# fp32 x1 product as one fp32r product over 96 stacked rows, and the class product over all 128 rows

## The chip, the cores and the metric

The kernel runs on one core of a Trainium2 chip. The time is the device time of one execution in microseconds (us), the median of three runs. Engines are named as the profile names them: PE (TensorE, matmuls; PEld are its weight loads), DVE (VectorE), ACT (ScalarE), POOL (GpSimd) and SP (SyncE, which issues most DMAs).

## The reference, cut to what matters

`x` has 128 entries of 64 positions and 256 features. Four layers follow one another. The change touches the first one and a table lookup in the last:

```python
def _L0_cond_ref(x, mu, W_dec, b_dec, V):          # K = 30
    U = (mu @ W_dec + b_dec).reshape(B, IN_DIM + 1, K)
    param = jnp.einsum('bik,kj->bij', U, V)
    weight = param[:, :-1, :]
    bias = param[:, -1, :]
    out = jnp.einsum('bsd,bde->bse', x, weight)
    out = out + bias[:, None, :]
    return out
...
x = x + _L0_cond_ref(x, cond_512, ...)             # x1 in the kernel
x = x + _L1_cond_ref(x, cond_512, ...)             # x2
x = _L2_cond_ref(x, ...)                           # x3
...
h = _ln(x, pw_g[pathway_ids], pw_b[pathway_ids])   # in the last layer, _L3_cond_ref
h = _ln(h, cp_g[compartment_ids], cp_b[compartment_ids])
t = _ln(x, tm_g[time_steps], tm_b[time_steps])
s = _ln(x, ms_g[scale_type], ms_b[scale_type])
```

The kernel computes layer 0 as t = x . U (30 values a position) and then x1 = x + t . V.

## The kernel before, in words

The 8192 positions are cut into 16 chunks of 512 (8 entries each). A tile holds either features on its 128 partitions (two blocks of 128 features by 512 positions) or positions (four tiles of 128 positions by 256 features). Setup decodes U for all entries and prepares tables; then each chunk goes through the stages in a software pipeline. Every engine has its own list of stages, written out by hand in `run_slots`: a list for the beginning, an `order` that a loop repeats for each chunk, each stage with a lag (the chunk it works on is the loop's number less the lag), and a list for the end. An engine runs its list strictly in that order and waits on semaphores that other engines raise. PSUM has four tensors of two banks, `ps_a` to `ps_d`, which the stages share in turn.

The stages that matter here, in the order in which a chunk meets them:

- `pe_t` (L919, TensorE): t for the 8 entries, into bank 1 of `ps_b`, four strips of 30 rows at partitions 0, 32, 64 and 96.
- `act_th1` (L1171, ScalarE) copies the four strips side by side into rows 0 to 29 of `t_st`; `act_th2` (L1178) copies those to rows 32 to 61.
- `pe_x1` (L935, TensorE): V times `t_st` into `ps_b`, in fp32. Feature block 0 uses rows 0 to 29, block 1 the copy in rows 32 to 61. The trace shows two passes (records) for each fp32 matmul. `v_x1add` (L1345) adds x.
- `g_style` (L1516, GpSimd) scales x1 into `xm_t`; `pe_l1` (L948) multiplies it in fp32 into `ps_d`; `v_l1mul`, `v_l1min` and `v_x2add` (L1352, L1361, L1367) make x2; `pe_dn` (L962), `v_dnmul`, `v_dnadd`, `act_relu`, `pe_up` (L976) and `v_x3sum` make x3.
- `pe_x3r` (L988) transposes x3, `v_xstat` (L1398) takes its statistics, `g_rootx` and `act_xnorm` normalise it, `g_gather` fetches table rows by an indirect DMA, `g_hmul` and `g_hadd` apply them, `v_hstat`, `g_rooth` and `act_hnorm` (L1209) normalise again.
- `pe_cp` (L1046, TensorE): the class gains as a product of one-hot rows (`onehot`) with `gain_tab`, in bf16, into `ps_d`. The 24 class rows stand twice in both operands, at partitions 0 and 64; position tiles 0 and 1 use the first copy, 2 and 3 the second. `v_hprod` (L1428) multiplies them onto h, `pe_hht` (L994) transposes h into `ps_b`, where t had been.
- The last layer's first product, 3 x 2 fp32r matmuls for each of 8 blocks (L902 to L904: low times high, high times low, high times high), in parts named x3, tm, ms and h; `act_silu`, `act_silh`, `v_sillow`; the second product `pe_w2` (the same lines into `ps_b`); `act_ysquare`, `g_rooty`, `v_ygain`, `v_ynorm` and the store.

"fp32r" is a fp32 type with a shorter mantissa, for which the trace shows one record a matmul; a value is split into a high half (a copy into fp32r) and a low half (value less high half), as the last layer does throughout.

The order of TensorE's loop is `pe_xht` 5, `pe_w1_tm` 6, `pe_up` 4, `pe_w1_ms` 6, `pe_cp` 5, `pe_x1` 3, `pe_w1_h` 6, `pe_x3r` 4, `pe_t` 2, `pe_l1` 3, `pe_hht` 5, `pe_shift` 5, `pe_w1_x3` 5, `pe_tm` 5, `pe_dn` 3, `pe_w2` 6, `pe_ms` 5 (the number is the lag). `pe_hht` waits, among others, for a semaphore that says that t has been read out of `ps_b`:

```python
        def pe_hht(eng, c):
            newest(eng, c, (v_x1, 2), (v_y, -2))
            newest(eng, c, (a_th1, 3), (v_x1, 2), (v_y, -2))
            wait(eng, v_h, c.n + 1)
```

## Time and profile before

| | us |
|---|---|
| median of three runs | 523.61 (521.86 to 524.25) |
| profiled execution, its own time | 521.21 |
| its span in the trace | 519.4 |
| mean granted TensorE clock | 0.994 of full speed |

| engine | busy us | share of the span | instructions |
|---|---|---|---|
| PE | 486.3 | 94% | 3198 |
| DVE | 405.8 | 78% | 696 |
| POOL | 391.0 | 75% | 367 |
| ACT | 336.3 | 65% | 638 |

Busy time of an engine is the time in which at least one of its instructions ran. Matmuls are pipelined: a record's duration holds the time until its last result is out, so the distance from one start to the next, and not the duration, is what a matmul costs in a row of them. The loop repeats every 27.8 us for each chunk in the middle of the span. "Idle" in brackets is time in which an engine had nothing running before an instruction, with the instruction or DMA whose end let it go.

### The profile page before, as it was taken

To read this page: it belongs to the slowest core of one execution; us is meant where nothing else is said; L and a number is where in the kernel's file an instruction comes from. 1 tells how busy PE (TensorE), PEld (TensorE's weight loads), DVE (VectorE), ACT (ScalarE), POOL (GpSimd) and SP (SyncE) were. 2 spreads that over 40 slices of the span, in tenths; PEclk is the share of its full clock that TensorE was granted. 3 is DMA by queue.
4 is the path that set the end of the run, shared out by engine and by line. 5 is a ranking of instruction groups with operands and counts; after the bars stand their busy time and mean duration, and the time that the engine had idled before them with its cause. 6 is when DMAs were issued, how large, how long until landed. Compare 5 with 4: busy or idle time off the path is not lost.

```text
span 519.4 us, 9425 instructions
## 1 busy us (share of the span) xinstructions
PE 486.3 (94%) x3198; PEld 354.2 (68%) x3198; DVE 405.8 (78%) x696; ACT 336.3 (65%) x638; POOL 391.0 (75%) x367
## 2 busy tenths in 40 slices
PE   2987887999999999999999999999999999998993
PEld 2953644767677776768686867677776768687682
DVE  2958876868788788888787878788787888886863
ACT  4573667456767676766777776767676767656832
POOL 6468799889878879697978787788779793787321
PEclk9999999999999999999999999999999999999997
DMA  8887705625252352608080716253442613104102
...
DMA packets 34989, 61.78 MB, mean 119 GB/s; under 512 B 5017, under 2 KB 17413, under 8 KB 34580
## 3 DMA queue, kind: packets, MB, share of 16 engines
...
q8 instruction: 14, 0.23, 0.2%
...
## 4 chain that ended last, share of the span: by engine, by line
PE 79%; POOL 6%; DVE 5%; DMA 4%; issue 3%; ACT 2%; SPq 0%; DVEq 0%; POOLq 0%; ACTq 0%
PE ps_c L902 11%; PE ps_c L904 11%; PE ps_c L903 10%; PE ps_d L948 9%; PE ps_d L962 5%; PE ps_a L976 5%; PE ps_b L902 3%; PE ps_b L903 3%; PE ps_b L904 3%; PE ps_b L935 2%; PE ps_a L988 2%; DMA set_wdec<-in_nets_rows 2%; PE ps_a L994 2%; PE ps_b L994 2%; DMA set_wdec<-in_W_dec 1%
## 5 line engine op out<-in xcount | busy, mean ns | idle before, releaser
L1507 POOL DMA_INDIRECT pw_rows<-in_pw,gidx x64 | 65.0, 1016 | 17.9 <-issue 17.4
L948 PE MATMUL ps_d<-xm_t,l_w 128*128 128x512 f32 x128 | 59.0, 603 | 2.2 <-POOL xm_t L1516 2.2
L1209 ACT ACTIVATE h<-h,nb_h,rstd_h 128x256 f32<-128x256 f32 x64 | 33.3, 591 | 33.1 <-POOL nb_h L1531 33.0
L1240 ACT ACTIVATE tm_t_h<-ps_a 128x1024 fp32r<-128x1024 f32 x16 | 16.4, 1026 | 45.6 <-DVE ps_a L1413 45.6
L1516 POOL TENSOR_TENSOR xm_t<-x_t,style 128x1024 f32<-128x1024 f32 x16 | 30.5, 1905 | 20.2 <-DVE x_t L1345 20.1
L948 PEld LDWEIGHTS ps_d<-xm_t,l_w 128*128 128x128 f32 x128 | 23.1, 190 | 26.8 <-issue 24.2
L1546 POOL TENSOR_TENSOR h<-xhat,pw_rows 128x1024 f32<-128x1024 f32 x16 | 38.0, 2378 | 4.1 <-ACT xhat L1209 4.1
L1565 POOL TENSOR_TENSOR w_up<-up_rep,ugub 128x1024 f32<-128x1024 f32 x16 | 38.0, 2372 | 2.2 <-issue 2.0
L1551 POOL TENSOR_TENSOR h<-h,pw_rows 128x1024 f32<-128x1024 f32 x16 | 38.3, 2394 | 1.3
L1567 POOL TENSOR_TENSOR w_up<-w_up,ugub 128x1024 f32<-128x1024 f32 x16 | 38.1, 2382 | 1.3
L902 PE MATMUL ps_b<-w_h,act_t_l 128*128 128x256 f32 x128 | 37.7, 294 | 0.4 <-DVE act_t_l L1450 0.4
L1577 POOL TENSOR_TENSOR x3be<-x,ln_gb 128x1024 f32<-128x1024 f32 x16 | 37.8, 2364 | 0.0
L1352 DVE TENSOR_TENSOR ps_d<-ps_d,dcoef 128x1024 f32<-128x1024 f32 x16 | 19.7, 1232 | 21.6 <-PE ps_d L948 21.6
L903 PE MATMUL ps_b<-w_l,act_t_h 128*128 128x256 f32 x128 | 36.1, 282 | 0.0
L904 PE MATMUL ps_b<-w_h,act_t_h 128*128 128x256 f32 x128 | 36.0, 281 | 0.0
L1209 ACT ACTIVATE xhat<-ps_a,nb_x,rstd_x 128x256 f32<-128x256 f32 x64 | 31.0, 564 | 6.7 <-POOL nb_x L1531 6.7
L962 PE MATMUL ps_d<-x_t,down_w 128*64 128x256 f32 x256 | 31.2, 385 | 3.0 <-DVE x_t L1367 3.0
L976 PEld LDWEIGHTS ps_a<-act_dn,w_up 128*128 128x128 f32 x256 | 30.5, 191 | 4.9 <-issue 2.6
L976 PE MATMUL ps_a<-act_dn,w_up 128*128 128x128 f32 x256 | 31.6, 277 | 2.2 <-ACT act_dn L1188 1.2
L1590 POOL TENSOR_TENSOR ve_y<-y_var,eps 128x4 f32<-128x4 f32 x15 | 3.0, 202 | 40.2 <-ACT y_sq L1320 40.2
L1418 DVE TENSOR_TENSOR ps_d<-ps_d,xh_t 128x1024 f32<-128x1024 f32 x16 | 19.7, 1231 | 17.4 <-PE ps_d L1031 17.4
L1320 ACT ACTIVATE y_sq<-ps_b 128x256 bf16<-128x256 f32 x64 | 23.7, 380 | 14.8 <-PE ps_b L904 14.8
...
## 6 DMA issues: line engine op xcount, KB each, us to landing
...
pw_rows<-in_pw,gidx POOLq DMA_INDIRECT x64, 3.7
...
```

The costliest lines, as they stand in the source:

```text
L902: eng.matmul(out, wl, ah, start=first, stop=False)
L903: eng.matmul(out, wh, al, start=False, stop=False)
L904: return eng.matmul(out, wh, ah, start=False, stop=last)
L948: m = eng.matmul(ps_l1[:, o, :], l1_w[:, k, o * P:(o + 1) * P], xm_t[:, k, :], start=k == 0, stop=k == KB - 1)
L962: m = eng.matmul(ps_dn[e * HID:(e + 1) * HID, part * CT * S:(part + 1) * CT * S], down_w[:, k, part * HID:(part + 1) * HID], x[:, k, e], s ...
L976: m = eng.matmul(ps_up[:, k, j * P:(j + 1) * P], w_up[:, j, k * P:(k + 1) * P], act_dn[:, j, :, :], start=True, stop=True)
L1209: m = eng.activation(out[:, j, :], src[:, j, :], ACT.Identity, bias=nb[k][:, j:j + 1], scale=rstd[k][:, j:j + 1])
L1507: eng.indirect_dma_start(pw_rows[c.ring][:, j, :], None, t["pw"], bass.IndirectOffsetOnAxis(ap=gidx[c.ring][:, j:j + 1], axis=0)).then_inc ...
L1546: eng.tensor_tensor(h1[:, :, :], xhat[:, :, :], pw_rows[c.ring][:, :, 0:D], ALU.mult).then_inc(g_h1m, 1)
L1551: eng.tensor_tensor(h1[:, :, :], h1[:, :, :], pw_rows[c.ring][:, :, D:2 * D], ALU.add).then_inc(g_h1, 1)
L1565: eng.tensor_tensor(w_up[:, :, :], q, ugub[:, :, 0:D], ALU.mult).then_inc(g_upm, 1)
L1567: eng.tensor_tensor(w_up[:, :, :], w_up[:, :, :], ugub[:, :, D:2 * D], ALU.add).then_inc(g_up, 1)
```

## The change

The fp32 product x1 becomes one fp32r matmul for each feature block, over 96 rows. `t_st` holds t's high half in rows 0 to 29, its low half in rows 32 to 61 and the high half again in rows 64 to 93; `v_st` holds V's high half in rows 0 to 63 and its low half from row 64. One pass then sums high times high, low times high and high times low. `act_th1` writes the high half, `act_th2` the copy of it, and a new stage on VectorE, `v_tlow`, takes the low half: four subtractions of 30 x 128 from the strips in `ps_b`. It stands before `v_l1mul` in VectorE's loop. `pe_x1` waits for both, and `pe_hht`, which overwrites the strips, waits for `v_tlow` in place of `act_th1`. In the setup `act_vhigh` and `v_vlow` split V, and `t_st` is set to zero once (rows 30, 31 and so on are never written).

`pe_cp` uses all 128 rows of `onehot` and `gain_tab`: columns 0 to 255 of `gain_tab` are zero outside the first 24 rows, so its four matmuls no longer use two copies of the class rows. Semaphores are merged where two can be one (`a_th1` into `a_th`, `v_l1u` and `v_l1v` into `v_l1`), with the same waits.

The diff, cut to its core (the semaphore lists and the waits of `v_l1min` and `v_x2add` are left out):

```diff
@@ -148,7 +148,8 @@
         later = sb("later", [CLS, PIECES - 1])
-        v_rep = sb("v_rep", [2 * RP, D])
+        v_rep = sb("v_rep", [PIECES * RP, D])
+        v_st = sb("v_st", [PIECES * RP, D], F32R)
         style = sb("style", [P, KB, B])
@@ -181,7 +182,7 @@
         act_dn = sb("act_dn", [P, CT, 2, S])
-        t_st = sb("t_st", [2 * RP, CH])
+        t_st = sb("t_st", [PIECES * RP, CH], F32R)
 
@@ -406,7 +407,7 @@
         rows_c = rows_of(ps_c)
-        pads = (ubias_p[:, :], act_dn[:, :, :, :], onehot[0][:, :], onehot[1][:, :], shift[0][:, :], shift[1][:, :], gain_tab[:, 2 * D:3 * D],)
+        pads = (ubias_p[:, :], act_dn[:, :, :, :], onehot[0][:, :], onehot[1][:, :], shift[0][:, :], shift[1][:, :], gain_tab[:, :], t_st[:, :].bitcast(F32),)
 
@@ -434,7 +435,7 @@
         def load_weights(eng, c):
-            eng.dma_start(v_rep[:, :], t["V3"][0:2 * RP, :]).then_inc(d_wts, 16)
+            eng.dma_start(v_rep[:, :], t["V3"]).then_inc(d_wts, 16)
             eng.dma_start(down_w[:, :, 0:HID], feat(t["down_p"])).then_inc(d_wts, 16)
@@ -595,6 +596,11 @@
 
+        def v_vlow(eng, c):
+            eng.wait_ge(c_v, 1)
+            low = slice(2 * RP, 3 * RP)
+            eng.tensor_tensor(v_st[low, :], v_rep[low, :], v_st[low, :].bitcast(F32), ALU.subtract).then_inc(c_v, 1)
+
         def v_awmax(eng, c):
@@ -667,8 +673,8 @@
             pick(eng, v_link, gain_tab[0:CLS, :], tab[1][:, :], *(p[:, :] for p in tab_p))
-            eng.scalar_tensor_tensor(gain_tab[STRIP:STRIP + CLS, 0:2 * D], tab_p[2][:, 0:2 * D], masks[:, 2:3],
-                                     tab[1][:, 0:2 * D], ALU.mult, ALU.add).then_inc(v_pick, 1)
+            eng.scalar_tensor_tensor(gain_tab[STRIP:STRIP + CLS, D:2 * D], tab_p[2][:, D:2 * D], masks[:, 2:3],
+                                     tab[1][:, D:2 * D], ALU.mult, ALU.add).then_inc(v_pick, 1)
 
@@ -700,6 +706,10 @@
                               ubias_p[:, e * RP:(e + 1) * RP]).then_inc(d_ub, 16)
+
+        def act_vhigh(eng, c):
+            eng.wait_ge(d_wts, 48)
+            eng.activation(v_st[:, :], v_rep[:, :], ACT.Copy).then_inc(c_v, 1)
 
@@ -929,10 +939,12 @@
             newest(eng, c, (v_y, -4), (v_hl, -3))
-            wait(eng, a_th, c.n + 1)
+            if first(c):
+                eng.wait_ge(c_v, 2)
+            wait(eng, a_th, 2 * c.n + 2)
+            wait(eng, v_thl, c.n + 1)
             for k in range(KB):
-                rows = slice(k * RP, k * RP + RK)
-                m = eng.matmul(ps_x1[:, k, :], v_rep[rows, k * P:(k + 1) * P], t_st[rows, :], start=True, stop=True)
+                m = eng.matmul(ps_x1[:, k, :], v_st[:, k * P:(k + 1) * P], t_st[:, :], start=True, stop=True)
             m.then_inc(p_x1, 1)
@@ -1041,16 +1053,14 @@
             out = rows_of(ps_cp)
-            for j in (0, 2, 1, 3):
-                rows = slice(j // 2 * STRIP, j // 2 * STRIP + CLS)
-                m = eng.matmul(out[:, j, :], onehot[c.ring][rows, j * P:(j + 1) * P], gain_tab[rows, 0:D],
-                               start=True, stop=True)
+            for j in range(CT):
+                m = eng.matmul(out[:, j, :], onehot[c.ring][:, j * P:(j + 1) * P], gain_tab[:, 0:D], start=True, stop=True)
             m.then_inc(p_cp, 1)
...
             newest(eng, c, (v_x1, 2), (v_y, -2))
-            newest(eng, c, (a_th1, 3), (v_x1, 2), (v_y, -2))
+            newest(eng, c, (v_thl, 3), (v_x1, 2), (v_y, -2))
             wait(eng, v_h, c.n + 1)
@@ -1164,18 +1174,20 @@
 
+            if first(c):
+                eng.wait_ge(z_pad, len(pads))
             wait(eng, p_t, c.n + 1)
...
                     "r (q s) -> r q s", s=S), ACT.Copy)
-            m.then_inc(a_th1, 1)
+            m.then_inc(a_th, 1)
 
...
 
-            wait(eng, a_th1, c.n + 1)
-            eng.activation(t_st[RP:RP + RK, :], t_st[0:RK, :], ACT.Copy).then_inc(a_th, 1)
+            wait(eng, a_th, 2 * c.n + 1)
+            eng.activation(t_st[2 * RP:2 * RP + RK, :], t_st[0:RK, :].bitcast(F32), ACT.Copy).then_inc(a_th, 1)
 
@@ -1337,6 +1349,15 @@
 
+        def v_tlow(eng, c):
+
+            wait(eng, a_th, 2 * c.n + 1)
+            high, out = (t_st[lo:lo + RK, :].rearrange("r (q j s) -> r q j s", j=4, s=S) for lo in (0, RP))
+            for j in range(4):
+                src = ps_t[j * RP:j * RP + RK, 0:2 * S].rearrange("r (q s) -> r q s", s=S)
+                m = eng.tensor_tensor(out[:, :, j, :], src, high[:, :, j, :].bitcast(F32), ALU.subtract)
+            m.then_inc(v_thl, 1)
+
         def v_x1add(eng, c):
@@ -1648,7 +1669,7 @@
...
-                             (act_turn, 12), (act_turn, 13), (act_turn, 15), (act_style, 0), (act_dg, 0),
+                             (act_turn, 12), (act_turn, 13), (act_turn, 15), (act_style, 0), (act_dg, 0), (act_vhigh, 0),
...
@@ -1685,23 +1706,23 @@
-                             (v_stylesq, 0), (v_softmax, 0), (v_dceps, 0), (v_dcrcp, 0), (v_x1add, 0),
-                             (v_mostat, 0), (v_w1sum, 0), (v_l1mul, 0), (v_l1min, 0), (v_x2add, 0), (v_monorm, 0),
+                             (v_stylesq, 0), (v_softmax, 0), (v_vlow, 0), (v_dceps, 0), (v_tlow, 0), (v_dcrcp, 0), (v_x1add, 0),
+                             (v_mostat, 0), (v_w1sum, 0), (v_l1mul, 0), (v_l1min, 0), (v_x2add, 0), (v_tlow, 1), (v_monorm, 0),
...
-                             (v_classes, 0), (v_l1mul, 1), (v_l1min, 1), (v_x2add, 1), (v_rows, 0), (v_dnmul, 1),
+                             (v_classes, 0), (v_l1mul, 1), (v_l1min, 1), (v_x2add, 1), (v_tlow, 2), (v_rows, 0), (v_dnmul, 1),
...
-                             (v_xstat, 1), (v_l1mul, 2), (v_l1min, 2), (v_x2add, 2), (v_tmprod, 0), (v_hlow, 0),
+                             (v_xstat, 1), (v_tlow, 3), (v_l1mul, 2), (v_l1min, 2), (v_x2add, 2), (v_tmprod, 0), (v_hlow, 0),
...
-                      order=[(v_x1add, 3), (v_hprod, 5), (v_xstat, 4), (v_sillow, 6), (v_l1mul, 3), (v_l1min, 3),
+                      order=[(v_x1add, 3), (v_hprod, 5), (v_xstat, 4), (v_sillow, 6), (v_tlow, 2), (v_l1mul, 3), (v_l1min, 3),
...
-                      end=[(v_x1add, 13), (v_hprod, 11), (v_xstat, 12), (v_sillow, 10), (v_l1mul, 13),
+                      end=[(v_x1add, 13), (v_hprod, 11), (v_xstat, 12), (v_sillow, 10), (v_tlow, 14), (v_l1mul, 13),
...
-                           (v_hprod, 12), (v_xstat, 13), (v_sillow, 11), (v_l1mul, 14), (v_l1min, 14),
+                           (v_hprod, 12), (v_xstat, 13), (v_sillow, 11), (v_tlow, 15), (v_l1mul, 14), (v_l1min, 14),
...

```

## Rows read from the trace of the kernel before

**Rows 1.** The page: the span, and busy time, share and instructions of each engine.
```profile
span 519.4 us, 9425 instructions
PE 486.3 (94%) x3198; PEld 354.2 (68%) x3198; DVE 405.8 (78%) x696; ACT 336.3 (65%) x638; POOL 391.0 (75%) x367
```

**Rows 2.** Stage table: stretch, length, busy us of PE, PEld, DVE, ACT, POOL; PEclk, DMA.
```profile
240.30:268.10 27.80, 27.80 (x187) 20.23 (x187) 23.10 (x39) 19.31 (x38) 22.43 (x20) 1.00 0.43 122
```

**Rows 3.** Timeline of TensorE in the first chunks: start, duration, line, shapes, count [idle].
```profile
56.10 1.13 PE L935 MATMUL ps_b<-t_st,v_rep 30*128 30x512 f32 x4
...
83.76 3.67 PE L948 MATMUL ps_d<-xm_t,l_w 128*128 128x512 f32 x8 [1.36 <-POOL xm_t L1516]
...
114.47 1.04 PE L994 MATMUL ps_b<-ident,h 128*128 128x128 f32 x8
```

**Rows 4.** Chain that ended last, 270 to 283 us: start, length, engine, tile, line.
```profile
272.20 0.21 PE ps_d L1046 x2
...
273.38 0.43 PE ps_c L902
273.82 0.23 PE ps_c L903
...
281.62 0.87 PE ps_b L994 x8
```

**Rows 5.** Timeline of TensorE in the loop: matmuls, then one weight load.
```profile
263.19 0.28 PE L904 MATMUL ps_b<-w_h,act_t_h 128*128 128x256 f32 x1
263.31 0.60 PE L1031 MATMUL ps_d<-onehot,gain_tab 128*128 128x512 bf16 x2
263.75 1.04 PE L994 MATMUL ps_a<-ident,xhat 128*128 128x128 f32 x8
...
260.57 0.19 PEld L904 LDWEIGHTS ps_b<-w_h,act_t_h 128*128 128x128 f32 x1
```

**Rows 6.** Timeline of VectorE in the loop; in brackets idle before, and its releaser.
```profile
275.90 1.22 DVE L1428 TENSOR_TENSOR h<-ps_d,h 128x1024 f32<-128x1024 f32 x1 [0.96 <-ACT h L1209]
277.28 1.42 DVE L1398 BATCH_NORM_STATS2 bn_x<-ps_a 128x6 f32<-128x256 f32 x4 [0.16 <-PE ps_a L988]
...
279.16 1.19 DVE L1437 TENSOR_TENSOR act_t_l<-ps_c,act_t_h 128x1024 fp32r<-128x1024 f32 x1
281.76 1.23 DVE L1352 TENSOR_TENSOR ps_d<-ps_d,dcoef 128x1024 f32<-128x1024 f32 x1 [1.41 <-PE ps_d L948]
...
288.06 0.43 DVE L1378 TENSOR_TENSOR ps_d<-ps_d,dgdb 128x256 f32<-128x256 f32 x1
288.40 0.41 DVE L1379 TENSOR_TENSOR dn_v<-ps_d,dgdb 128x256 f32<-128x256 f32 x1
```

**Rows 7.** Timeline of VectorE in the setup and the first chunks.
```profile
8.15 1.20 DVE L587 COPY set_w_rt<-set_wdec 128x512 f32<-128x512 f32 x2 [5.72 <-DMA set_wdec<-in_W_dec]
...
12.33 0.20 DVE L397 TENSOR_TENSOR ps_b<-ps_b,set_ubias_p 128x30 f32<-128x30 f32 x1
...
33.57 1.75 DVE L624 RECIPROCAL set_dm<-set_dm 128x256 f32<-128x256 f32 x1 [2.32 <-ACT set_dm L733]
...
48.51 1.45 DVE L641 TENSOR_SCALAR ps_c<-ps_c,set_mo_mv,set_mo_r 128x256 f32<-128x256 f32 x3
...
70.88 0.41 DVE L396 CAST set_rowb_p<-ps_c 128x256 bf16<-128x256 f32 x1
...
87.47 1.23 DVE L1352 TENSOR_TENSOR ps_d<-ps_d,dcoef 128x1024 f32<-128x1024 f32 x1 [2.64 <-PE ps_d L948]
```

**Rows 8.** Timeline of ScalarE in the loop: the copies of `act_th1`.
```profile
278.66 1.10 ACT L1171 ACTIVATE t_st<-ps_b 30x128 f32<-30x128 f32 x4
```

**Rows 9.** Timelines of ScalarE and GpSimd in the setup and first chunks.
```profile
27.76 1.05 ACT L1163 ACTIVATE u_ch<-u_all 128x480 f32<-128x480 f32 x1 [2.81 <-DVE u_all L595]
...
81.70 1.91 POOL L1516 TENSOR_TENSOR xm_t<-x_t,style 128x1024 f32<-128x1024 f32 x1
...
112.68 1.10 ACT L1171 ACTIVATE t_st<-ps_b 30x128 f32<-30x128 f32 x4
```

20 lines of the change are left out of this document (10 added, 10 removed).

## The prediction, made before the kernel was changed

> **What bounds the kernel now.** I read the page's busy shares and slices first, then the stage table, then TensorE's part of the chain that ended last, then VectorE's and ScalarE's timelines beside it. TensorE is busy 486.3 of 519.4 us [rows 1], and a stretch of exactly a loop period (27.8 us) in the middle of the span has it busy for its whole length at a granted clock of 1.00 (the upper of its two levels, 2.4 GHz), with VectorE at 23.10, ScalarE at 19.31 and GpSimd at 22.43 of the 27.80 [rows 2]. Between 129 and 440 us TensorE's waits name nobody. So between about 93 us (chunk 2's down product) and about 470 us the end moves with TensorE's own time, chunk by chunk; what the other engines do counts there only if it comes late for TensorE. Before 93 us it is otherwise: TensorE waits in turn for VectorE, ScalarE and GpSimd (the last of these waits is 1.36 us for `xm_t` of chunk 2) [rows 3], and there a longer VectorE moves the end.
>
> **TensorE's part.** The two products that change stand side by side, `pe_cp` and then `pe_x1`, between the `ms` and the `h` parts of the last layer's first product. The chain gives their true length. The `ms` part's last matmul ends at 272.20; cp and x1 run until 273.38; then the first `h` matmul takes 0.43 where its neighbours take 0.23, so 0.20 us of it belongs to the change of array layout. Together: 273.38 - 272.20 + 0.20 = 1.38 us per chunk [rows 4]. (The four x1 passes are two fp32 products of two passes each, on rows 0-29 and 32-61, side by side; the four cp matmuls run in two pairs, on rows 0-23 and 64-87.)
> After the change: four bf16 matmuls of 128 rows x 256 columns and two fp32r ones of 96 rows x 512 columns, one after the other. Neither shape is in the trace. For the fp32r ones the nearest rows are the `h` products (128 rows, fp32r, 512 columns), 0.23 us from start to start [rows 4]; moving columns, not rows, set a matmul's length here, so I take 2 x 0.23 = 0.46. For the cp ones two rows bound the cost: the class product ms (128 rows, bf16, 512 columns) takes 263.75 - 263.31 = 0.44 for two, which is 0.11 per 256 columns; the second layer's fp32r products with 256 columns follow each other every 0.12 (L904 at 263.19, the next matmul at 263.31) [rows 5]. So 0.44 to 0.48, and I take 0.46. The 0.20 of the layout change goes, since nothing here leaves the full array any more: the ms pair enters straight behind a full-array product at its usual pitch [rows 5]. Sum 0.92 (0.90 to 0.94) against 1.38: **0.46 us less per chunk** (0.44 to 0.48; down to 0.40 if 96 rows count as a layout of their own and half of the 0.20 doesn't go, though no row shows such a step between shapes that use the whole array).
> Where does that count? x1 of chunks 3 to 15 stands in the stretch that TensorE bounds: 13 x 0.46 = 6.0 us. In front of it x1 of chunks 0 to 2 has no cp beside it; cp of chunk 0 ends ahead of a wait of 1.36 us [rows 3], so it is free. Behind x1 of chunk 15, cp of chunks 14 and 15 stand alone and lose their pairing: two pairs of 0.11 become 0.46, with a layout change of about 0.1 (half of the 0.20) gone, so about 0.1 each; I put one of them on the path: +0.1.
>
> **VectorE's part, in the loop.** The new `v_tlow` is four subtractions of 30 x 128 from PSUM per chunk. The trace has no such form. Above: a 128 x 256 one at 0.43 [rows 6], so 1.7 us for four. Below: a 128 x 30 one at 0.20 [rows 7], so 0.8 us. Between two of these 256-wide ones the start moves by only 0.34 (288.40 - 288.06) [rows 6]; half the columns take off 128 / 256 of the part that grows with them, about 0.13 (0.43 - 0.20 over 226 columns is 0.001 us a column). That makes 0.30 for one and 0.21 from start to start: 3 x 0.21 + 0.30 = **0.93 us**.
> It stands between `v_sillow` and `v_l1mul`. There VectorE now idles 1.41 us for TensorE's l1 product [rows 6], so 0.93 fits. But two things move. First, TensorE arrives 0.46 earlier. Second, a new wait: `pe_hht` now waits for `v_tlow` (it overwrites the bank that v_tlow reads) where it waited for ScalarE's `act_th1`, done at 278.66 + 1.10 = 279.76 [rows 8]. Behind pe_hht on TensorE's queue stand the shift, the x3 part of the last layer, tm, down and the second layer: everything waits. So the cover is this. pe_hht starts at 281.62 now [rows 4] and at 281.16 after. VectorE: `v_hprod` starts at 275.90 behind ScalarE's `act_hnorm` [rows 6], which a GpSimd chain (root, gather, root) releases and not TensorE's products, so I let it stay. xstat would follow its 1.22 (pitch about 1.14) at 277.04 in place of 277.28, as the transposes it waits for come earlier; sillow 1.88 later, at 278.92; v_tlow 1.13 later, at 280.05 (act_th1 is done by then), and ends at 280.98. That is 0.18 ahead of pe_hht, and v_l1mul, which waits for l1 as before, isn't late either. Cost: nothing, with a thin cover: v_tlow may take 1.11 us before TensorE stalls (less a few hundredths for the semaphore, 1.06).
> `act_th2` keeps its form; x1's own wait for v_tlow comes most of a period after it. The six edits to semaphores (l1u and l1v merged and so on) cost nothing.
>
> **Setup and first chunks.** The memsets of the whole `gain_tab` and of `t_st` lie in VectorE's 5.72 us of idle before W_dec lands [rows 7]: free. `act_vhigh` (96 x 256; like the 0.43 of VectorE for that width) waits for the three weight loads and lies in ScalarE's 2.81 us of idle ahead of `act_u` of chunk 0 [rows 9]. That is free; were the loads late, x1 of chunk 0 would be late, and it has VectorE's wait for the square root behind it (next sentence). `v_vlow` and v_tlow of chunk 0 lie in the idle ahead of the reciprocal (2.32 us), v_tlow of chunk 3 in that ahead of v_l1mul of chunk 2 (2.64 us) [rows 7]. The other two have no cover: v_tlow of chunk 1 comes ahead of `v_monorm` (L641) at 48.51, and that of chunk 2 ahead of `v_rows` (L396) at 70.88, and neither row shows idle [rows 7]. Each pushes VectorE by 0.93. The first reaches TensorE by relu and up; x1 of chunk 1 (1.13 us, alone) [rows 3] shrinks to 0.46 right behind, so some 0.3 is left. The second reaches chunk 0's h statistics and ScalarE's relu, thus GpSimd's `xm_t` of chunk 2 at 81.70, for which TensorE waits [rows 3, 9]: up to 0.93, of which x1 of chunk 2 gives a little back on one of the two ways. Between 0 and 2 x 0.93 = 1.86, I take **+1.1 us**.
> One more place is late once: with chunk 4 ScalarE still runs `act_x3` ahead of `act_th1`, which ends at 112.68 + 1.10 = 113.78 [rows 9]; v_tlow behind it would end at 114.71, while the h transposes start at 114.47 [rows 3]. Both follow TensorE's `h` part, so the gap stays: **+0.3 us** (0 to 0.4).
>
> **Sum.** -6.0 + 0.1 + 1.1 + 0.3 = -4.5 us. The profiled execution's own time is 521.21 (span 519.4 and 1.8 around it), so it would be 516.7; the median of the three runs is 523.61, 2.40 above the profiled one, and the median after is 523.61 - 4.5 = **519.1 us**.
>
> **Rivals.**
> A, *slower: v_tlow overruns.* Mechanism: pe_hht waits for VectorE in every chunk. Above 1.06 us each further 0.1 of v_tlow costs TensorE 0.1; from 1.06 + 0.46 = 1.52 us on the change loses. At the upper end, 1.7, a chunk grows by 0.18, 12 x 0.18 = 2.2, and the first chunks by about 2.5: 528.3. For it: the 0.43 row and a cover of under 0.2. Against it: width counts, as the 0.20 row shows.
> B, *no change: the side chain holds the period.* GpSimd's chain to hnorm doesn't shrink, and the cover that I worked out is 0.1 to 0.2 us. If the semaphores on the way and GpSimd's own variation take 0.3 us more than that, TensorE keeps only 0.15 to 0.2 of its 0.46: 13 x 0.18 = 2.3, less 1.5: 522.8. For it: VectorE already waits for hnorm (0.96) [rows 6]. Against it: pe_hht, the first to notice, doesn't wait at all now.
> C, *the products aren't shorter: weights load in the open.* Each of the six matmuls would show its weight load. In the trace a full-array load of 0.19 us lies in full under matmuls that follow each other every 0.12 [rows 5], which is why I give it little. Priced with that 0.19 for each: 6 x 0.19 = 1.14 more than 0.92, 2.06 against 1.38, 13 x 0.68 = 8.8 lost, and 1.5: 533.9.
> The Trainium skill, page "TensorE: Matmul & The Clock Gate", section "Part 3: Packing small matmuls — row/col tiling", would have C: it says that LDWEIGHTS overlaps with matmuls in flight only when their row groups differ, and that small-K products gain by sharing the array, which is what this change gives up. By that rule the time is C's; the rows just named disagree with it.
> D, *more than forecast*: the late steps of the first chunks are absorbed and a chunk gives 0.48: 13 x 0.48 = 6.2, 517.4.
>
> **How the numbers follow.** Forecast 0.60, D 0.12, B 0.17, A 0.08, C 0.03. The range: forecast with its bounds (13 x 0.40 less 1.9, 0.4 and 0.2 gives 520.9; 13 x 0.48 less 1.5 gives 518.9), D at 517.4, B at 522.8, and about 1 us on each side since the three runs of before differ by 2.4: 516.4 to 523.4. It leaves out A, C and a bit of B. A measurement of this kernel tells 0.5% (2.6 us) from no change, so faster means below 521.0: forecast, D and a sliver of B, 0.75; same, most of B: 0.15; slower, A, C and what of B ends there: 0.10.
>
> **What the profile after would show.** Right: from the end of the ms part to the start of the h part 0.90 to 0.94 us, and the first h matmul at 0.23; L948 of neighbouring chunks 27.3 us apart in place of 27.8; no wait of TensorE for `t_st` from VectorE; VectorE idle ahead of v_l1mul down from 1.41 to about 0.3; four subtractions in 0.93 us; chunk 2's down product about 1.1 us later than now. Wrong: v_tlow over 1.06 us and a wait of the h transposes for VectorE (A), such a wait with v_tlow at 0.93 (B), cp matmuls 0.3 us apart (C), or the chunk 2 shift near 0 or 2 us.

## The result

The changed kernel is slower. Its median is 531.48 us over six executions (527.00 to 532.04) against 523.51 us over six of the kernel before (521.86 to 524.25); the ratio is 1.0127, 95% interval 1.0091 to 1.0163. On another chip the same pair (run `e10_after` below) gave 523.87 against 521.88 us, ratio 1.0048 (1.0013 to 1.0084). The sign is the same, the size is not, and part of the study is why. The forecast was 519.1 us. Of the changed kernel's six executions two took 527.0 and 527.1 us and four 531.3 to 532.0. Only one of the faster two was traced, so the trace accounts for 5.8 of the 8.0 us between the medians.

The profiled execution took 527.0 us (span 525.2) where that of before took 521.21 (span 519.4): 5.8 us more. The page of after, to be held against [rows 1]; the last line is the granted clock in tenths, by fortieths of the span:

```profile
span 525.2 us, 9483 instructions
PE 484.5 (92%) x3166; PEld 359.9 (69%) x3166; DVE 424.3 (81%) x762; ACT 336.0 (64%) x639; POOL 389.5 (74%) x367
...
PEclk9999899998999999999999999999999999999997
```

TensorE has 1.8 us less work than in [rows 1], half-clock time included, and yet the span grew: it now waits. VectorE has 18.5 us more, about 16 times the new `v_tlow`.

Where the time went is seen from the starts of the first layer's product (`pe_l1`), one for each chunk, read from TensorE's timeline:

| start of l1, us | chunk 0 | 1 | 2 | 3 | 4 | 12 | 15 | span |
|---|---|---|---|---|---|---|---|---|
| before | 40.25 | 63.38 | 83.76 | 110.93 | 138.99 | 361.23 | 443.86 | 519.4 |
| after | 40.32 | 65.26 | 86.91 | 113.63 | 144.95 | 367.61 | 449.92 | 525.2 |
| difference | +0.07 | +1.88 | +3.15 | +2.70 | +5.96 | +6.38 | +6.06 | +5.8 |

So the whole loss of this execution arises before 145 us, and the loop gives nothing back: from chunk 4 to chunk 12 a period was 27.78 us before and is 27.83 after, where 27.78 - 0.46 = 27.32 was forecast. I take the loop first.

**The products got shorter as forecast.** The chain that ended last, around the two products (start, length, engine, tile, line; L1057 is `pe_cp`, L947 `pe_x1`, L912 the first product of the `h` part):

```profile
306.40 0.23 PE ps_c L914
306.64 0.45 PE ps_d L1057 x4
307.09 0.46 PE ps_b L947 x2
307.55 0.23 PE ps_c L912
```

0.91 to 0.92 us from the end of the ms part to the start of the h part, and the first h product takes 0.23, not 0.43: against [rows 4] the change takes 0.46 off this stretch.

**And `pe_hht` gives it back.** VectorE and TensorE in the same period (start, duration, line, shapes, count, idle before):

```profile
285.62 1.19 DVE L1458 TENSOR_TENSOR act_t_l<-ps_c,act_t_h 128x1024 fp32r<-128x1024 f32 x1
286.84 1.19 DVE L1358 TENSOR_TENSOR t_st<-ps_b,t_st 30x128 fp32r<-30x128 f32 x4
288.06 1.23 DVE L1373 TENSOR_TENSOR ps_d<-ps_d,dcoef 128x1024 f32<-128x1024 f32 x1
...
284.18 3.70 PE L960 MATMUL ps_d<-xm_t,l_w 128*128 128x512 f32 x8
288.13 1.06 PE L1006 MATMUL ps_b<-ident,h 128*128 128x128 f32 x8 [0.25 <-issue]
```

`v_tlow` (L1358) takes 1.19 us. The transposes of h (L1006) start 0.10 after its end. That is 3.95 us after l1's start; in the kernel before it was 3.53, from this timeline:

```profile
277.92 3.70 PE L948 MATMUL ps_d<-xm_t,l_w 128*128 128x512 f32 x8
281.45 1.04 PE L994 MATMUL ps_b<-ident,h 128*128 128x128 f32 x8
```

TensorE's waits between 145 and 440 us (total, times, longest) were none before. Now there is this one, and a single wait of 0.2 us beside it:

```profile
PE ps_b L1006 <- issue: 2.9, 9, 0.4
```

The profile names "issue" and not VectorE for it; that it is the wait for `v_tlow` is what the first group of experiments shows.

**The front.** TensorE's timeline:

```profile
52.96 0.85 PE L544 MATMUL ps_c<-ident,set_mo 128*128 128x128 f32 x6 [2.75 <-DVE set_mo L651]
55.01 3.25 PE L988 MATMUL ps_a<-act_dn,w_up 128*128 128x128 f32 x16 [1.21 <-ACT act_dn L1200]
```

And the stage table for the stretches behind this wait and behind a later one (busy time of PE, PEld, DVE, ACT, POOL; then the granted clock):

```profile
55.00:58.50 3.50, 3.49 (x18) 3.39 (x18) 2.53 (x4) 3.48 (x5) 1.96 (x3) 0.58 1.04 231
120.40:123.80 3.40, 3.40 (x11) 2.50 (x9) 3.33 (x5) 2.85 (x5) 3.32 (x2) 0.50 0.00 0
```

The wait for `set_mo` was 1.41 us and is 2.75. Behind it TensorE's granted clock falls to 0.5, the lower of its two levels (1.2 GHz), for some 3 us, and the first up product takes 3.25 us where it took 2.02. In the trace of before there was no such stretch ahead of 510 us. After has a second one, at chunk 4 (the second row). There the timelines of ScalarE and TensorE read:

```profile
117.13 1.11 ACT L1183 ACTIVATE t_st<-ps_b 30x128 fp32r<-30x128 f32 x4 [1.65 <-remote]
...
119.56 1.14 PE L1006 MATMUL ps_b<-ident,h 128*128 128x128 f32 x8 [2.23 <-issue]
```

ScalarE was free for `act_th1` of chunk 4 at 115.5 but started it at 117.13, though `pe_t` of that chunk had ended at 113.70. The trace's record of semaphore updates shows that `pe_t`'s signal came only at 117.11, as the l1 product behind it was ending (117.33). So `v_tlow` came late, the h transposes waited 2.23 us, and the clock fell.

### The profile page after: what moved, and what is told of

It reads as the page before. It is cut to its first block, busy times and chain, and to the rows that moved or that the text cites. A ratio compares the mean times of both kernels' runs of the same rounds, so it can differ in the third digit from the quotient of the medians.

```text
span 525.2 us, 9483 instructions
## 1 busy us (share of the span) xinstructions
PE 484.5 (92%) x3166; PEld 359.9 (69%) x3166; DVE 424.3 (81%) x762; ACT 336.0 (64%) x639; POOL 389.5 (74%) x367
## 4 chain that ended last, share of the span: by engine, by line
PE 74%; DVE 8%; issue 5%; POOL 4%; ACT 4%; DMA 3%; SPq 0%; ACTq 0%; DVEq 0%; POOLq 0%
PE ps_d L960 10%; PE ps_c L912 10%; PE ps_c L914 10%; PE ps_c L913 10%; PE ps_d L974 5%; PE ps_a L988 5%; PE ps_b L912 3%; PE ps_b L913 3%; PE ps_b L914 3%; PE ps_b L1006 3%; PE ps_a L1000 2%; PE ps_a L1006 2%; DMA set_wdec<-in_W_dec 1%; PE ps_b L929 1%; DMA ub_scratch<-set_ubias_p 1%
## 5 line engine op out<-in xcount | busy, mean ns | idle before, releaser
L1528 POOL DMA_INDIRECT pw_rows<-in_pw,gidx x64 | 63.4, 991 | 17.8 <-issue 17.7
L912 PE MATMUL ps_b<-w_h,act_t_l 128*128 128x256 f32 x128 | 37.7, 295 | 0.4 <-DVE act_t_l L1471 0.4
L988 PE MATMUL ps_a<-act_dn,w_up 128*128 128x128 f32 x256 | 32.8, 283 | 3.5 <-ACT xh_t L1242 2.3
L988 PEld LDWEIGHTS ps_a<-act_dn,w_up 128*128 128x128 f32 x256 | 31.6, 197 | 6.2 <-ACT xh_t L1242 2.8
L912 PE MATMUL ps_c<-x_t_h,w_l 128*128 128x512 f32 x64 | 29.2, 456 | 0.0
```

The source lines that it names most:

```text
L912: eng.matmul(out, wl, ah, start=first, stop=False)
L988: m = eng.matmul(ps_up[:, k, j * P:(j + 1) * P], w_up[:, j, k * P:(k + 1) * P], act_dn[:, j, :, :], start=True, stop=True)
L1528: eng.indirect_dma_start(pw_rows[c.ring][:, j, :], None, t["pw"], bass.IndirectOffsetOnAxis(ap=gidx[c.ring][:, j:j + 1], axis=0)).then_inc ...
```

## The experiments

Each "before" below is the kernel before on the same chip as the kernels beside it.

**First group: which part, and what holds the loop.** `e1_cp` and `e2_x1` each make one half of the change alone:

```diff
# e1_cp: kernel before, with only the class product over all 128 rows (the lines that fill gain_tab left out)
-            for j in (0, 2, 1, 3):
-                rows = slice(j // 2 * STRIP, j // 2 * STRIP + CLS)
-                m = eng.matmul(out[:, j, :], onehot[c.ring][rows, j * P:(j + 1) * P], gain_tab[rows, 0:D],
+            for j in range(CT):
+                m = eng.matmul(out[:, j, :], onehot[c.ring][:, j * P:(j + 1) * P], gain_tab[:, 0:D], start=True, stop=True)
# e2_x1: kernel after, with these lines (and gain_tab) put back
```

> The kernel before with the class product's part of the change alone (all 128 rows, zeros); x1 stays fp32. No v_tlow, so neither theory has a wait here. From the ms part's end to the start of the h part: 0.45 us of cp, then x1 alone about 1.05 to 1.13, and the layout steps of 0.1 on each side: 1.6 to 1.7 us against 1.38. So 13 x 0.25 = 3.3 us slower than before, about 527, with TensorE still busy throughout and a period near 28.05 us.

> The changed kernel with cp put back on its two strips of rows; x1 in fp32r over 96 rows and v_tlow stay. cp should take 0.2 plus two layout steps of 0.1, x1 0.46: 0.88 in all, as good as the changed kernel's 0.92. Theory W (the h transposes wait for v_tlow and that holds the period): 27.8 us a period as in the changed kernel, 527 to 532 in all, the same losses in the first chunks. If the cp part were the harm instead, it would be near 519.

`e1_cp`: 529.36 us median (525.30 to 533.18) against 524.33; ratio 1.0075 (1.0032 to 1.0118). Its period is 28.11, 0.33 more than before, a little above the 0.25 expected: by itself the class product only loses its pairing. `e2_x1`: 528.31 us (526.52 to 532.62), ratio 1.0081 (1.0046 to 1.0116); period 27.81. Its chain shows the two products with the class one on two strips of rows:

```profile
306.12 0.32 PE ps_d L1058 x4
306.45 0.66 PE ps_b L947 x2
307.11 0.24 PE ps_c L912
```

0.98 us for the pair, against 0.92 with both edits and 1.38 before. So x1's edit brings 0.40 and cp's, which costs 0.33 alone, brings another 0.06 once x1 is on the full array: the 0.20 of the layout change sits inside x1's 0.66, which is 0.46 behind a full-array product. Yet the period is that of after to 0.02 us. TensorE's work is not what sets it.

`e3_low1` does one of `v_tlow`'s four subtractions and leaves the low half of six of a chunk's eight entries out. `e4_loop` keeps all work and only reorders:

```diff
# e3_low1
-            for j in range(4):
+            for j in range(1):
                 src = ps_t[j * RP:j * RP + RK, 0:2 * S].rearrange("r (q s) -> r q s", s=S)
# e4_loop: ScalarE's and VectorE's orders (the closing lists alike, and act_th1 of chunk 4 in ScalarE's opening list)
-  (act_silu, 5), (act_gidx, 1), (act_silh, 5), (act_th1, 1)
+  (act_silu, 5), (act_th1, 1), (act_gidx, 1), (act_silh, 5)
-  (v_sillow, 6), (v_tlow, 2), (v_l1mul, 3)
+  (v_tlow, 2), (v_sillow, 6), (v_l1mul, 3)
```

> The changed kernel with v_tlow doing one of its four subtractions (the low half of six of the eight entries' t is left out of x1). Theory W: v_tlow falls from 1.19 to about 0.3 us, the h transposes no longer wait, the period falls by 0.4 to 0.46 to 27.3 to 27.4 us, and with two steps of 0.9 in the first chunks gone the time is 518 to 521. Theory G (GpSimd's chain through the gather holds the period whatever v_tlow takes): the period stays at 27.8 and the time is about 525 to 530.

> The changed kernel with another order in the loop alone: ScalarE runs act_th1 ahead of act_silh, and VectorE v_tlow ahead of v_sillow, whose result TensorE needs only some 9 us later. Nothing is left out. Theory W: v_tlow ends about 0.9 us ahead of the h transposes, the period is 27.3 to 27.4 us, 12 x 0.4 = 5 us less than the changed kernel, so 521 to 525 (first chunks unchanged). Theory G: 27.8 us, 527 to 532. If v_l1mul, now behind both, comes late for the down product, the wait shows there instead.

`e3_low1`: 517.99 us (517.54 to 520.15), ratio 0.9864 (0.9807 to 0.9920), period 27.31. `e4_loop`: 526.03 (522.88 to 528.37), ratio 1.0010 (0.9970 to 1.0050), period 27.32. In both the h transposes follow l1 at once. `e3_low1` and then `e4_loop`:

```profile
280.29 0.28 DVE L1358 TENSOR_TENSOR t_st<-ps_b,t_st 30x128 fp32r<-30x128 f32 x1
281.48 1.23 DVE L1373 TENSOR_TENSOR ps_d<-ps_d,dcoef 128x1024 f32<-128x1024 f32 x1 [0.91 <-PE ps_d L960]
...
281.17 1.04 PE L1006 MATMUL ps_b<-ident,h 128*128 128x128 f32 x8
```

```profile
288.29 1.19 DVE L1358 TENSOR_TENSOR t_st<-ps_b,t_st 30x128 fp32r<-30x128 f32 x4
...
286.71 3.70 PE L960 MATMUL ps_d<-xm_t,l_w 128*128 128x512 f32 x8
290.25 1.04 PE L1006 MATMUL ps_b<-ident,h 128*128 128x128 f32 x8
```

From l1 to the transposes it is 3.54 us in both, as before the change (3.53). That settles the loop: it is the wait for `v_tlow` (theory W). The chain through GpSimd (theory G) would have held the period at 27.8 in both, and did not. `e4_loop` shows too that the loop is not all: its period is 0.5 us shorter, yet at 526.03 it missed the 521 to 525 us expected. Its l1 of chunk 4 starts at 150.09, with half-clock stretches at 56, 84 and 125 us.

*Another delay in the front.* One more thing differs there, and it is none of the changes. VectorE's step on `ps_c` and `set_wdec` waits for a load by DMA. It starts between 39.4 and 40.9 us in twelve of the traces (40.92 in before, 40.19 in after), and at 42.5 to 43.8 in four: `e3_low1`, `e4_loop`, `e13_keepwarm` and `e14_front`. In those four the first down product starts at 50.3 to 51.6 us, where the others have it at 47.7 to 48.7. `e9_front` and then `e14_front`, the same kernel:

```profile
40.93 0.96 DVE L635 TENSOR_TENSOR ps_c<-ps_c,set_wdec 128x768 f32<-128x768 f32 x1 [3.83 <-DMA set_wdec<-in_nets_rows]
...
43.79 0.97 DVE L635 TENSOR_TENSOR ps_c<-ps_c,set_wdec 128x768 f32<-128x768 f32 x1 [6.58 <-DMA set_wdec<-in_nets_rows]
```

So starts in the front of these four are not to be held against the others' without taking off these 2 to 3 us. Why the load is late in them is open.

**Second group: the front.** `e5_setup` moves `v_tlow` of chunks 1 and 2 behind VectorE's urgent work, `e6_both` adds `e4_loop`'s order, `e7_warm` fills TensorE's idle time, and `e8_before` is the kernel before again.

```diff
# e5_setup (e6_both: the same, with e4_loop's orders)
-  (v_x2add, 0), (v_tlow, 1), (v_monorm, 0), (v_dnmul, 0), (v_dnadd, 0), (v_gains, 0)
+  (v_x2add, 0), (v_monorm, 0), (v_dnmul, 0), (v_dnadd, 0), (v_tlow, 1), (v_gains, 0)
-  (v_x2add, 1), (v_tlow, 2), (v_rows, 0), (v_dnmul, 1), (v_dnadd, 1), (v_hstat, 0)
+  (v_x2add, 1), (v_rows, 0), (v_dnmul, 1), (v_dnadd, 1), (v_hstat, 0), (v_tlow, 2)
# e7_warm: kernel after, ten more products by ones in a fifth pe_warm
-  (pe_dn, 0), (pe_mot, 0), (pe_up, 0)
+  (pe_dn, 0), (pe_warm, 4), (pe_mot, 0), (pe_up, 0)
```

> The changed kernel with two steps moved in VectorE's list for the first chunks alone: v_tlow of chunk 1 from ahead of v_monorm to behind v_dnadd of chunk 0, and v_tlow of chunk 2 from ahead of v_rows to behind v_hstat of chunk 0. The loop is as in the changed kernel. Theory E (the loss against the kernel before lies ahead of 145 us and begins with VectorE's new steps there): v_monorm ends about 1.2 us earlier, TensorE's wait for set_mo is 1.4 to 1.6 us again instead of 2.75, no stretch of half clock follows it, and the second and third l1 start near 63.5 and 84.5 us instead of 65.26 and 86.91; the time is 523 to 525 us, with the loop's period still near 27.83. Rival F (the early loss is an accident of how the chip's clock fell in that execution, or belongs to the later stall of act_th1 for chunk 4): the l1 starts of chunks 1 and 2 stay within 0.5 us of 65.26 and 86.91, and the time stays at 527 or above.

> The changed kernel with both rearrangements: in the loop act_th1 ahead of act_silh and v_tlow ahead of v_sillow (as in e4_loop), and for the first chunks v_tlow of chunk 1 behind v_dnadd of chunk 0 and that of chunk 2 behind v_hstat of chunk 0 (as in e5_setup). Theory W with E (two separate losses, each with its own remedy, which add): the loop's period is 27.3 to 27.35 us and the l1 of chunk 2 starts near 84.5 us; the time is 517 to 520 us, below both kernels. If the stall of act_th1 for chunk 4 stays, that costs about 3 us of it and the time is 519 to 522. Rival: the loss at the front only moves (a half-clock stretch falls at another place); the period is 27.3 but the l1 of chunk 4 starts near 149 us, and the time is 524 to 527.

> The changed kernel with nothing but ten more warming products (128x512 by a matrix of ones, about 0.23 us each, results unused) on TensorE between the first down product and the transposes of set_mo, where TensorE stood idle for 2.75 us ahead of a stretch at half clock. Theory C (the half clock that follows the idle time is a loss of its own, 1.2 us, the time that the first up product takes more: 3.25 instead of 2.02 us): no half-clock stretch at 55 to 58 us, up(0) takes 2.0 us, the second l1 starts 1.0 to 1.4 us earlier (near 64 us), and the time falls by 1 to 1.5 us, to near 526 for an execution whose other stretches are as in the changed kernel. Rival: the clock falls all the same, or the set-up chain and not TensorE sets the pace there; the second l1 still starts at 65.2 us and the time is as that of the changed kernel.

> The kernel before, unchanged, looked at a second time. In every changed kernel so far TensorE's signal that the projection of chunk 4 is done came 3.4 to 3.7 us after its last product ended, just as the first layer product of chunk 3 ended, and act_th1 of chunk 4 waited for it; in the one trace of the kernel before it came after 0.1 us. Theory P (the late signal belongs to the changed programs): this trace shows no late signal at chunk 4, and act_th1 of chunk 4 starts near 112.7 us. Theory X (the late signal comes in some executions of any of these kernels and not in others): this trace shows it too, act_th1 starts near 114.8 us, and the span is 2 to 4 us above 519.4 us.

Medians, with 524.42 us for before: `e5_setup` 526.08 (523.03 to 526.73), ratio 1.0030 (0.9998 to 1.0062); `e6_both` 523.13 (519.48 to 525.00), ratio 0.9971 (0.9934 to 1.0007); `e7_warm` 526.72 (525.34 to 529.55), ratio 1.0056 (1.0021 to 1.0092).

*A miss, and a find.* `e5_setup` brings the wait for `set_mo` back to 1.41 us, but its second l1 starts at 66.16, not at 63.5, and its time is above the 523 to 525 expected. Something new is in the way. In `e6_both`, VectorE's last `gain_tab` step, GpSimd beside it, and TensorE:

```profile
56.95 2.62 DVE L676 SCALAR_TENSOR_TENSOR gain_tab<-set_tab_p,cls_const,set_tab 24x256 bf16<-24x256 bf16 x1
...
56.92 2.37 POOL L851 TENSOR_TENSOR w_l<-set_wdec,w_h 128x1024 fp32r<-128x1024 f32 x1
...
60.98 1.07 PE L1000 MATMUL ps_a<-ident,x_t 128*128 128x128 f32 x8 [2.11 <-DVE x_t L1413]
```

In the kernel after that step takes 0.48 us, at 56.90, ahead of the same GpSimd operation at 57.90. Here the GpSimd operation comes 1 us earlier, but the step does not, since `v_tlow` of chunk 1 now stands ahead of it. So it falls beside GpSimd's and lasts until that one is done; TensorE waits 2.11 us, and a half-clock stretch follows at 62 us. `e6_both` as a whole, at 523.13, lies between what its two theories allowed (522 at most, and 524 at least). `e7_warm` does what it should at its place: no half clock at 55 us, up(0) in 2.02, the second l1 at 64.02. But a stretch of half clock came at 80 us instead (0.50 from 80.3 to 87.1), and the third l1 starts at 86.95, where after had 86.91. Theory C is right on the price at the place (1.24 us at the second l1), but the gain is gone by the third. The medians can't be used for the sum, as the kernel after was not run beside it.

*The late signal belongs to no kernel.* ScalarE in `e8_before`, the kernel before, unchanged:

```profile
114.42 1.11 ACT L1171 ACTIVATE t_st<-ps_b 30x128 f32<-30x128 f32 x4 [1.92 <-remote]
```

The same late signal, 3.67 us behind `pe_t`'s last product. Of the theories of this run that leaves X, though the span, at 520.4 us, is only 1.0 above the first trace's and not 2 to 4. From l1 of chunk 3 to that of chunk 4 it has 29.25 us, where the first trace of before had 28.06: the late signal costs the kernel before 1.2 us. After pays more, since there `v_tlow` stands between `act_th1` and the transposes, and since the clock can fall behind the wait: that step is 29.79 us in `e7_warm`, with the late signal and no fall, and 31.32 in after, with both.

Two things about the place, from the same records. `pe_t` of chunk 4 is the first that TensorE runs from the loop; those of chunks 0 to 3 stand in the opening list. And each trace with the late signal at chunk 4 has one at chunk 1 too, by 1.3 to 1.5 us, and at no other chunk (0.03 to 0.05 us). The one at chunk 1 cost nothing in after: `act_th1` ended at 47.17, and `v_tlow` started at 48.15, right behind `v_x2add`. Whether the entry into the loop has to do with the delay, no run tells.

**Third group: mending the front.** `e9_front` is `e6_both` with `v_tlow` of chunk 1 behind `v_gains`, and `pe_x1` of chunk 1 behind the class products. `e11_all` also moves `pe_t` ahead of `pe_x3r`. `e10_after` is the kernel after.

```diff
# e9_front, on top of e6_both
-  (v_tlow, 1), (v_gains, 0)
+  (v_gains, 0), (v_tlow, 1)
-  (pe_up, 0), (pe_x1, 1), (pe_cls, 0), (pe_x3r, 0)
+  (pe_up, 0), (pe_cls, 0), (pe_x1, 1), (pe_x3r, 0)
# e11_all, on top of e9_front, in loop and closing list
-  (pe_w1_h, 6), (pe_x3r, 4), (pe_t, 2), (pe_l1, 3)
+  (pe_w1_h, 6), (pe_t, 2), (pe_x3r, 4), (pe_l1, 3)
```

> e6_both with two more moves at the front: v_tlow of chunk 1 goes behind v_gains (in e6_both it stood ahead of it, and the last gain_tab step then ran beside GpSimd's w_l step and took 2.62 instead of 0.48 us), and on TensorE pe_x1 of chunk 1 goes behind pe_cls. Theory Q (that overlap with GpSimd, 2.1 us, is what the moves of e5_setup and e6_both lost again, and the idle time of TensorE that it makes, 2.11 us, is what the half-clock stretch at 62 us follows): the last gain_tab step ends before 57 us and takes 0.5 us, there is no half-clock stretch before 100 us, the l1 of chunk 1 starts at 62.5 to 63.5 us and that of chunk 2 at 83 to 84 (86.49 in e6_both), and the time is 2.5 to 3.5 us below e6_both's 523.13, so 519.5 to 520.5. Rival: another step takes its place (x1 of chunk 1 now comes late for v_x1add), the second l1 starts at 65 us or later and the time stays at 522 to 524.

> The changed kernel itself, unchanged, beside e9_front and e11_all on one chip. Its profiled execution had two half-clock stretches and took 527.0 us; four of its six executions took 531.3 to 532.0 us at a mean granted clock of 0.981, which no trace has shown. Theory D (the groups of times are numbers of half-clock stretches): executions at a granted clock of 0.988 take 526 to 528 us, those at 0.981 take 530 to 532, and if the profiled one is of the second kind its trace shows about four stretches ahead of the last one. Rival: the times spread without following the granted clock.

> e9_front, and on TensorE the projection pe_t goes ahead of pe_x3r in the loop and in the closing list, so that 1.04 us of other work lies between it and l1. It asks what TensorE's late signal at chunk 4 hangs on. Theory L (the signal of pe_t comes only as the group of products behind it ends): with x3r behind it the signal of chunk 4 comes about 1 us after its last product, act_th1 of chunk 4 starts 3 to 3.5 us before the end of l1 of chunk 3, pe_hht waits no longer there, the half-clock stretch near 120 us is gone, and the time is 3 to 4 us below e9_front. Rival M (the signal is late by itself, by 3.5 us or until l1 ends): act_th1 of chunk 4 starts within 1 us of where it did (just as l1 of chunk 3 ends, or 1 us before), and the time is within 1 us of e9_front's.

With 521.88 us (520.40 to 528.92) for before: `e9_front` 517.09 (515.38 to 520.17), ratio 0.9879 (0.9820 to 0.9937), period 27.33; `e10_after` 523.87 (523.30 to 528.32), ratio 1.0048 (1.0013 to 1.0084); `e11_all` 522.16 (521.71 to 527.92), ratio 1.0016 (0.9973 to 1.0059).

None of the three traces shows the late signal. In `e10_after` the step from l1 of chunk 3 to that of chunk 4 is 27.92 us, in after it was 31.32: the late signal and what followed it took 3.4 of the 5.8 us. The front, though, cost more in this trace: its third l1 starts at 89.74 us, 5.98 behind before where after was 3.15 behind. The wait for `set_mo` is the same 2.75, but the half-clock stretch behind it is twice as long (54 to 61 us), and a second one follows at 81. `e9_front`'s `gain_tab` step is at 56.08 and takes 0.48, as theory Q has it. Its trace nevertheless has a stretch of half clock from 53 to 60 us, with up(0) at 3.76, another at 94, and the second l1 at 65.80. `e11_all`, with the same lists for the front, has none and starts it at 62.46, where theory Q wanted it. So with the clock held the mended front starts the second l1 at 62.46 (63.38 in the kernel before, 66.16 in `e6_both`), and `e9_front` starts it 3.3 us later; 0.7 of that was there at the first l1 (40.77 against 40.10), so the fall of the clock takes 2.7. Whether it falls is not the same in every execution. `e10_after` puts a number to it: its executions at a mean granted clock of 0.988 to 0.992 took 523.3 to 524.0 us, those at 0.984 and 0.985 took 526.5 to 528.3. That the times follow the granted clock is as theory D has it; the times themselves are not, as it had 526 to 528 us at 0.988. They are some 3 us lower, about what the missing late signal is worth.

`e11_all` can't tell L from M, for want of a late signal. It lost the loop for another reason (TensorE's waits, 145 to 440 us):

```profile
PE ps_c L1084 <- DVE act_t_l L1458: 6.2, 10, 1.3
```

With `pe_t` first, x3r's statistics reach VectorE later, `v_sillow` moves back, and now the shift product waits for it: period 27.88.

**Last group: VectorE's time by itself, and the idle gap by itself.**

```diff
# e12_spare: kernel before, with spare adds at the two places
+        def v_spare(eng, c):
+            eng.wait_ge(d_id, 16)
+            wide = ident[:, :].unsqueeze(1).broadcast_to([P, 2, P])
+            for _ in range(3):
+                v_link(eng.tensor_tensor(spare[:, :, :], wide, wide, ALU.add))
-  (v_x2add, 0), (v_monorm, 0)          (v_x2add, 1), (v_rows, 0)
+  (v_x2add, 0), (v_spare, 0), (v_monorm, 0)     (v_x2add, 1), (v_spare, 1), (v_rows, 0)
# e13_keepwarm: e9_front, five more products by ones
-  (pe_dn, 0), (pe_mot, 0), (pe_up, 0)
+  (pe_dn, 0), (pe_warm, 4), (pe_mot, 0), (pe_up, 0)
```

> The kernel before with spare work on VectorE and nothing else: three adds of 128x256 elements, whose result nobody reads, ahead of v_monorm and again ahead of v_rows, the two places where the changed kernel has v_tlow of chunks 1 and 2. Each group should take 1.3 to 1.4 us, a little more than v_tlow's 1.19. Theory S (VectorE's time at those two places is the cause of the early loss, and the x1 product itself has no part in it): TensorE's wait for set_mo grows from 1.41 to 2.7 us or more, a half-clock stretch follows near 55 us in most executions, the l1 of chunk 1 starts at 65.5 to 66.8 us (63.38 before) and that of chunk 2 at 87 to 90 (83.76 before), and the time is 3 to 6 us above the kernel before. Rival: the front has slack for VectorE and the loss in the changed kernel came from its other new work there (act_vhigh, v_vlow, the later x1); the l1 of chunk 2 starts before 85.5 us and the time is within 1.5 us of before.

> e9_front with five more warming products (128x512, 0.23 us each, results unused) on TensorE between the first down product and the transposes of set_mo, where e9_front leaves it idle for 1.41 us; its trace had a half-clock stretch of double length from 53.3 us, right behind that gap, in which up(0) took 3.76 instead of 2.02 us and the class products 3.91 instead of 2.77. Theory K (that gap is what lets the clock fall): no half-clock stretch between 50 and 66 us, the l1 of chunk 1 starts at 62.3 to 62.8 us, and the time is 515 to 517.5 us with less spread than e14_front's. Rival: e11_all had the same gaps (0.85, 1.41 and 1.21 us) and no such stretch, so that the gap alone does not decide; the median lies within 1 us of e14_front's.

> e9_front again, unchanged, on the chip of the two others, as their yardstick and as a second measurement of a version below both kernels. Expected: 516 to 519.5 us, ratio to before 0.985 to 0.993, the loop's period 27.33 us. If TensorE's late signal of chunk 4 is there on this chip (act_th1 of chunk 4 starting as l1 of chunk 3 ends), the time is 1.5 to 3 us higher, at 519 to 521.

With 524.51 us (522.57 to 529.69) for before: `e12_spare` 535.76 (534.76 to 537.38), ratio 1.0212 (1.0150 to 1.0274); `e13_keepwarm` 520.73 (518.59 to 521.88), ratio 0.9917 (0.9890 to 0.9944); `e14_front` 521.77 (519.09 to 524.50), ratio 0.9918 (0.9878 to 0.9958).

`e12_spare` missed its size, since the spare work did. VectorE, GpSimd and TensorE:

```profile
48.42 3.78 DVE L603 TENSOR_TENSOR spare<-ident 128x256 f32<-128x256 f32 x3
76.52 6.25 DVE L603 TENSOR_TENSOR spare<-ident 128x256 f32<-128x256 f32 x3
...
77.48 2.53 POOL L1572 TENSOR_TENSOR w_up<-up_rep,ugub 128x1024 f32<-128x1024 f32 x1
80.09 2.41 POOL L1574 TENSOR_TENSOR w_up<-w_up,ugub 128x1024 f32<-128x1024 f32 x1
...
55.83 1.51 PE L544 MATMUL ps_c<-ident,set_mo 128*128 128x128 f32 x6 [5.24 <-DVE set_mo L652]
```

Three adds that should take 1.3 us took 3.78 and 6.25. Both inputs of an add are in SBUF, and beside GpSimd's operations on SBUF tensors an add waits until one of them has ended: the second group is done at 82.77, 0.3 us behind the GpSimd operation that ends at 82.50. The direction is plain all the same, and theory S stands: 3.78 us ahead of `v_monorm` make TensorE wait 3.83 more (5.24 against 1.41), and the second l1 is 5.65 late; both groups, 10.03 us, make the fifth l1 14.3 late (153.31 against 138.99), half-clock stretches at 55 and 86 us and a late signal included. The front has no slack for VectorE at these two places, and the changed product isn't needed for the loss. What 1.19 us there cost by themselves this run doesn't tell, as its groups are three and five times that.

`e13_keepwarm` has no half clock between 50 and 66 us and up(0) in 2.02; `e14_front` has a stretch at 57 us and 3.54. Eight of ten executions of `e13_keepwarm` had a granted clock of 0.991 or 0.992, four of ten of `e14_front`. The medians differ by 1.0 us, at the edge of what its expectation allowed the rival, and the ranges overlap. So the counts and the times point to a rarer fall, worth about 1 us, but ten executions of each don't show it. Both kernels missed their expected times (515 to 517.5 us, and 519 to 521 with the late signal). Both have the late load of `set_wdec`: TensorE waited 2.66 and 3.41 us for `v_x2add` ahead of the first down product, a wait of 0.64 in `e9_front`, and that is why the second l1 of `e13_keepwarm` came only at 64.99. Less the 2.1 us by which its down product is later than that of `e9_front` (50.80 against 48.74) it is 62.9, near the 62.3 to 62.8 expected. Both have the late signal and a stretch of half clock at chunk 4 (118 and 122 us).

## Why the prediction was wrong

**TensorE's part: right.** Forecast 0.92 us for the two products and 0.23 for the first h product; measured 0.91 to 0.92 and 0.23. C is refuted: the class matmuls follow each other at 0.11 and x1's two take 0.46, and their weight loads (0.10 and 0.19) lie under the matmuls ahead of them. The rule cited from the Trainium skill ("TensorE: Matmul & The Clock Gate", "Part 3: Packing small matmuls — row/col tiling"), by which loads in the same row groups are exposed, does not describe this trace. What that section says of sharing the array holds in `e1_cp`: the unpaired class product alone costs 0.33 a chunk.

**VectorE's part in the loop: the step that failed.** Two of its terms were off, both to the same side.
- *v_tlow's size.* One subtraction was taken at 0.30 and measures 0.28. But I let the next start after 0.21, as the 256-wide pair of L1378 and L1379 overlaps in [rows 6]. These don't: (1.19 - 0.28) / 3 = 0.30 from start to start. So it was 1.19 instead of 0.93, inside the upper bound of 1.7. Why these don't overlap is not shown: they differ from that pair in width, in type and in that each reads another strip of partitions.
- *The cover.* I counted from the chain's start of the transposes (281.62), which books them behind the end of l1. The timeline has them start at 281.45, 3.53 after l1. `v_sillow` came where I said (1.44 after l1 instead of 1.46), `v_tlow` 1.22 behind it instead of 1.13, and 0.10 goes from its end to TensorE. So the cover was 3.53 - 2.66 - 0.10 = 0.77, not 1.06. By rival A's own price a `v_tlow` of 1.19 would have cost 0.13 a chunk; it cost 1.19 - 0.77 = 0.42 at this place, and 0.51 in the period (27.83 against 27.32); the other 0.09 has no place in these rows. The 0.46 saved is gone.

What happened is A's mechanism, which I gave 0.08; in the loop it ate the saving and no more. B's own cause, GpSimd's chain, is refuted by `e3_low1` and `e4_loop`. I also held A to need 1.52 us before it loses; with the true cover it needs 1.23, and 1.19 is next to that.

**Setup and first chunks: right place, wrong size.** The two uncovered `v_tlow` were named, with +1.1 and at most 1.86. By chunk 2's l1 the loss is 3.15. The waits grew at the places named, the first by 2.75 - 1.41 = 1.34. But a half-clock stretch followed the longer wait, up(0) took 3.25 instead of 2.02, and no term stood for that. `e7_warm`, and `e11_all` held against `e9_front`, show it to be a loss of its own: 1.2 and 2.7 us. `e10_after`, 5.98 us late at the same place, shows that a size read from one trace is not that of the next.

**Chunk 4: +0.3 forecast, +3.26 measured.** I let `v_tlow` be late behind `act_x3`. Without the late signal the step is 0.14 shorter than before (27.92 against 28.06), and -0.46 + 0.3 = -0.16 was forecast, so the size of that term was right. With the late signal the step is 3.26 longer, and no term stood for it. The trace of before had no late signal, and I could not know of it from there; but that execution, at 521.21 us faster than each of the timed ones (521.86 at least), was also free of half-clock stretches in its front, and I should have asked what the others had. **Tail**: +0.1 forecast, -0.26 measured.

Put together: forecast -6.0 + 0.1 + 1.1 + 0.3; measured, by the table, about +0.1 (chunk 4 to 15, where 11 x 0.46 = 5.1 was to be saved) - 0.26 + 3.15 - 0.45 (chunk 2 to 3) + 3.26 = +5.8.

**Expected of the profile after**: right on the products, and right in what it named as the sign of A, `v_tlow` over 1.06 us and a wait of the h transposes for VectorE. VectorE's idle time ahead of `v_l1mul` is gone where about 0.3 us was expected. Chunk 2's down product starts at 94.62 us instead of 91.47, 3.15 later and not 1.1.

**What stays open.** Why TensorE's signal for `pe_t` of chunk 4 comes 3.2 to 3.7 us late in some runs. The first trace of after and all traces of three groups have it, whatever the kernel; none of the third group does, nor the first trace of before. The groups ran on different chips at different times, and no experiment here separates the two. And why the clock falls behind the same gap in one execution and not in the next. The four executions of after at a granted clock of 0.981 (531.3 to 532.0 us) were never traced; that they have more half-clock time is an inference from their clock. The nearest traces point the same way: ahead of the last stretch after has 6.8 us of half clock at 0.988, `e10_after` 10.2 at 0.984 and `e4_loop` 13.6 at 0.982. Not tried: giving t a bank of its own, which would free the transposes from `v_tlow` altogether.
